# Second attention: the next image's transposes and projections one slot earlier, statistics in slot 10 of the image before

## The reference

```
xn = layer_norm(x) * scale + offset                      # per position, 192 channels
q, k, v = xn @ wq + bq, xn @ wk + bk, xn @ wv + bv       # 12 heads of 48
logits = q @ k.T / sqrt(48) + bias_h(q, rel_pos_0) + bias_w(q, rel_pos_1)
out = softmax(logits) @ v                                # 256 x 256 per head and image
x2 = x + (out @ wo + bo)
```

## Time and profile before

| | us |
|---|---|
| median of three runs (lowest, highest) | 853.67 (852.67, 854.36) |
| the profiled execution, its own time | 853.72 |
| its span, first to last instruction | 851.9 |
| PE busy in the span | 762.1 (89%) |
| DVE busy | 528.4 (62%) |
| ACT busy | 435.5 (51%) |
| POOL busy | 129.8 (15%) |

### The profile page before, as it was taken

How to read it: one execution, slowest core, us unless ns; L and a number is a source line. 1 busy time by engine, 2 the same in 40 slices (tenths; PEclk the granted TensorE clock), 3 DMA queues, 4 the chain that set the end, 5 groups by cost and what they waited for, 6 DMA issues and landing times.

```text
span 851.9 us, 18544 instructions
## 1 busy us (share of the span) xinstructions
PE 762.1 (89%) x6570; PEld 614.5 (72%) x6570; DVE 528.4 (62%) x1592; ACT 435.5 (51%) x1421; POOL 129.8 (15%) x243
## 2 busy tenths in 40 slices
PE   3779889898989887799979999999999999997998
PEld 2557566575756664589967787878787878775998
DVE  6155866767576777567426676766666666675551
ACT  2025655656465564455435555555555555654442
POOL 7200111011010110033330101010101010100221
PEclk9569999999899998799997999999999999999999
DMA  7321621010102100100040404040404040400001
GB/s 142 60 54 31 165 36 21 17 24 14 32 6 37 19 19 1 36 3 1 2 75 1 76 1 75 2 75 1 76 1 76 1 76 1 76 1 1 20 20 38
DMA packets 39147, 30.06 MB, mean 35 GB/s; under 512 B 12662, under 2 KB 37010, under 8 KB 39056
## 3 DMA queue, kind: packets, MB, share of 16 engines
q1 hardware_dynamic: 36030, 26.55, 16.8%
q0 software_dynamic: 2048, 1.89, 1.2%
q10 hardware_dynamic: 978, 0.43, 0.3%
HBM read 8.77 MB, written 1.57 MB: 12 GB/s over the span
## 4 chain that ended last, share of the span: by engine, by line
PE 75%; DVE 12%; issue 4%; ACT 3%; DMA 3%; SPq 1%; ACTq 1%; POOL 1%; DVEq 0%; POOLq 0%
PE bank L1284 10%; PE bank L1370 8%; PE bank L536 7%; PE bank L516 7%; PE bank L1311 5%; PE bank L1159 5%; PE bank L1291 4%; PE bank L966 4%; PE bank L1330 4%; PE bank L990 4%; PE bank L1091 3%; PE bank L1426 3%; DVE Pb L718 3%; DVE nmax L697 2%; PE bank L1017 2%
## 5 line engine op out<-in xcount | busy, mean ns | idle before, releaser
L707 ACT ACTIVATE Pb<-bank,nmax 128x256 f32<-128x256 f32 (+1 forms) x432 | 192.4, 453 | 89.6 <-DVE nmax L697 86.8
L697 DVE TENSOR_REDUCE nmax<-bank 128x2 f32<-128x392 f32 (+2 forms) x240 | 138.7, 579 | 45.2 <-PE bank L1284 33.0
L718 DVE TENSOR_SCALAR Pb<-Pb,rsum 128x196 f32<-128x196 f32 (+2 forms) x432 | 136.8, 354 | 8.5
L737 ACT COPY area<-bank 98x392 f32<-98x392 f32 (+1 forms) x144 | 77.5, 539 | 84.1 <-PE bank L1291 71.9
L1284 PE MATMUL bank<-QK 80*128 80x256 f32 x384 | 107.7, 405 | 9.6 <-DMA QK<-rel_dense 7.4
L1284 PEld LDWEIGHTS bank<-QK 80*128 80x128 f32 x384 | 69.1, 198 | 30.8 <-issue 14.6
L707 ACT ACTIVATION_READ_ACCUMULATOR Pb<-bank,nmax 128x1 f32 x432 | 87.4, 202 | 0.0
L990 PE MATMUL bank<-ident,Pb 128*98 128x128 f32 x384 | 64.2, 292 | 20.7 <-DVE Pb L718 20.7
L525 ACT ACTIVATE area<-bank,fc1b 128x256 f32<-128x256 f32 x96 | 45.2, 476 | 55.7 <-PE bank L516 48.2
L990 PEld LDWEIGHTS bank<-ident,Pb 128*98 128x98 f32 x384 | 41.6, 133 | 35.1 <-DVE Pb L718 29.9
L536 PE MATMUL bank<-fc2w,area 128*128 128x192 f32 x384 | 64.7, 326 | 0.0
(11 more groups left out here) (151 smaller groups left out, 1494.4 us busy)
## 6 DMA issues: line engine op xcount, KB each, us to landing
QK<-dense SPq DMA_DIRECT2D x32, 288.0 KB, 6.2
QK<-dense SPq DMA_DIRECT2D x48, 64.0 KB, 2.4
QK<-dense SPq DMA_DIRECT2D x90, 28.0 KB
QK<-rel_dense SPq DMA_DIRECT2D x32, 48.0 KB, 3.3
QK<-rel_dense POOLq DMA_DIRECT2D x32, 48.0 KB, 3.0
out<-x_all SPq DMA_DIRECT2D x8, 192.0 KB, 2.0
x_all<-in_x SPq DMA_DIRECT2D x1, 1344.0 KB, 17.0
QK<-in_c_hot SPq DMA_DIRECT2D x2, 384.0 KB, 5.0
```

The source lines that it names most:

```text
L697: nc.vector.tensor_reduce(nmax[0:sc.shape[0], u % 3, 0:sc.shape[1]], sc, AX.X, ALU.max, negate=True).then_inc(self.m_rdy, 1)
L707: nc.scalar.activation(Pb[u % 3][0:rows, t, 0:cols], sc[:, t, :], ACT.Exp, bias=nmax[0:rows, u % 3, t:t + 1], accum_out=esum[0:rows, u % 3 ...
L718: nc.vector.tensor_scalar(Pb[u % 3][0:rows, t, 0:keep], Pb[u % 3][0:rows, t, 0:keep], rsum[0:rows, u % 3, t:t + 1], None, ALU.mult).then_i ...
L737: copy(*self.pt_views(u)).then_inc(self.pt[self.pt_engine(u)], 1)
```

## The change

All front work of the second attention from `xhat` on moves one slot forward, in the same lumps: `xhat` into slot 0, the transposes of x and both halves of the normalized x into slot 1, q and k in slots 2, 3 and 4 (the last with the position products), the copies into `rel_dense` in slot 5, v in slots 6 and 7. The statistics move from slot 0 of an image to slot 10 of the image before it, two images ahead of their use; those of image 1 are taken at the start of the stage. POOL makes `rstd` accordingly behind `xbias` of two images before, and no longer ahead of the four DMAs. No instruction is added or taken away. The first attention keeps its order.

```diff
                 slot = {"pe": self.pe_slot, "act": self.act_slot, "dve": self.dve_slot}[which]
+                if which == "dve" and self.STATS_SLOT is not None:
+                    self.dve_stats(eng, Img(0, 1))
                 for k in sorted(fronts):
-                    if started and k <= 2:
+                    if started and k <= self.XT_SLOT:
                         continue
...
-                if u == 2 and ahead(self.NU - 1, 1):
+                if u == self.XT_SLOT and ahead(self.NU - 1, 1):
                     self.pe_transpose_x(eng, n.next())
...
-                if u == 1 and ahead(self.NU - 1, 1):
+                if u == self.XT_SLOT - 1 and ahead(self.NU - 1, 1):
                     self.dve_xhat(eng, n.next())
                 if u == self.VALUES_BEHIND and has_prev:
                     self.dve_back(eng, n.prev())
+                if u == self.STATS_SLOT and 2 * n.pair + n.par + 2 < B:
+                    self.dve_stats(eng, n.next().next())
...
         class Attention1(Attention):
+            XT_SLOT = 1
+            STATS_SLOT = 10
-            V_SLOT = 7
+            V_SLOT = 6
...
-                self.dve_fronts = {0: [self.dve_stats], 1: [self.dve_xhat], 2: [self.dve_xn], 3: each(self.dve_k, (0, 1, 2)),
+                self.dve_fronts = {0: [self.dve_xhat], 1: [self.dve_xn], 2: each(self.dve_k, (0, 1, 2)),
...
+            def run_pool(self, eng, following, after_front):
+                self.norm.pool_rstd(eng, Img(0, 1))
+                self.pool_front(eng, Img(0, 0))
+                after_front(eng)
+
+                def step(n, has_prev, has_next):
+                    if has_next:
+                        self.pool_front(eng, n.next())
+                    else:
+                        following(eng)
+                    self.pool_xbias(eng, n)
+                    if 2 * n.pair + n.par + 2 < B:
+                        self.norm.pool_rstd(eng, n.next().next())
+                image_loop(eng, step)
```

More of the change, by code:

```diff
@@ L924, in build @@
         class Attention0(Attention):
+            XT_SLOT = 2
+            STATS_SLOT = None
             G_USES = (6, 5)
@@ L1518, in setup @@
                 self.xl = sem("a1_xl")
[L1519 to L1524, removed]
@@ L1525, in setup @@
-                self.dve_fronts = {0: [self.dve_stats], 1: [self.dve_xhat], 2: [self.dve_xn], 3: each(self.dve_k, (0, 1, 2)),
-                                   4: each(self.dve_k, (3, 4)), 5: each(self.dve_k, (5,)), 6: [self.dve_rel],
-                                   7: each(self.dve_v, (0,)), 8: each(self.dve_v, (1,))}
+                self.pe_fronts = {1: [self.pe_transpose_x], 2: each(self.pe_qk, (0, 1, 2)), 3: each(self.pe_qk, (3, 4)),
+                                  4: each(self.pe_qk, (5,)) + [self.pe_rel], 6: each(self.pe_v, (0,)),
+                                  7: each(self.pe_v, (1,))}
@@ new lines, in setup @@
+                self.act_fronts = {1: [self.act_xn], 2: each(self.act_q, (0, 1, 2)), 3: each(self.act_q, (3, 4)),
+                                   4: each(self.act_q, (5,)), 5: [self.act_rel], 6: each(self.act_v, (0,)),
+                                   7: each(self.act_v, (1,))}
+                self.dve_fronts = {0: [self.dve_xhat], 1: [self.dve_xn], 2: each(self.dve_k, (0, 1, 2)),
+                                   3: each(self.dve_k, (3, 4)), 4: each(self.dve_k, (5,)), 5: [self.dve_rel],
+                                   6: each(self.dve_v, (0,)), 7: each(self.dve_v, (1,))}
@@ L1695, in _ @@
                 nc.gpsimd.memset(v[:, :, :, D1:64], 0.0).then_inc(prep_pool, 1)
-            a1.run_pool(pool, following=lambda e: m1.norm.pool_rstd(e, Img(0, 0)), started=True,
+            a1.run_pool(pool, following=lambda e: m1.norm.pool_rstd(e, Img(0, 0)),
                         after_front=lambda e: m1.low_weights(e, nc.gpsimd))
```

## The result

The changed kernel took **846.97 us** in the median of 10 runs (845.11 to 851.35), against 854.42 of the kernel before on the same chip in 10 runs (852.67 to 858.14): ratio 0.991, with a 95% interval of 0.989 to 0.9929. Its profiled execution took 846.04 us, with a span of 844.2 (before: 853.72 and 851.9); PE is busy for 756.5 us of it (90%).

The account below looks back on a forecast made before the run. PE's instruction stream plus its waits was taken to bound the second attention. Terms -5.4, -0.7, +1.8 and +0.1 sum to -4.2 on 853.72, giving 849.5 us; range 847.8 to 853.2.

Parts of the forecast that it names:

- signs: Profile after: no slot 9 waits, some 0.3 us at q, 41.5 us between images, DVE's wait about 0.5, clock 1.00.
- Slot 9, -5.4: Slot 9's scores: all seven waits, put down to late scatters out of rel_dense, go, saving 5.4 us.
- 0.3 to 0.9 early: Slot 9: scatters that came 0.44 to 1.03 us late would come 0.3 to 0.9 us early.
- The new wait at q, +1.8: q behind the values: PE waits 0.3 us in each of six images for a 2.7 us chain from residual to q.
- Sequence costs, -0.7: PE's order of scores and products: one costlier case fewer per image, -0.1 us for each of seven images.
- xhat: xhat in slot 0 on DVE, ahead of PE's transposes of x: cost 0, bounds 0 to 0.1 us for seven images.
- statistics: Statistics in slot 10 on DVE: 1.0 us covered by 1.46 us of idle time, cost 0.
- the start: Start of the stage: image 1's statistics ahead of the first copy of k cost +0.1 us, bounds 0 and 0.4.
- POOL against DVE: DVE's norm colliding with POOL's xbias moves a slot forward; 1.1 us remain before the transposes, so cost 0.
- The longer chain: Rival: wait at q of 0.7 to 1.0 us in six images, 851.9 to 853.7 us; chance 14%.
- a kept wait in slot 9: Rival: slot 9's wait stays in part, through exponentials or late landings, 850.5 to 852.5 us; chance 8%.
- The clock: Rival: pauses at q drop PE's granted clock, up to 859.7 us; slower by pause or clock, chance 8%.

Follow-up runs that it names:

- e9: Kernel before, with the q and k transfers issued in two parts, heads 0 to 5 as soon as copied: 845.7 us, ratio 0.9894.
- e2: The changed kernel, unchanged, run again beside the kernel before: 849.12 us, ratio 0.9947.
- e12: The changed kernel with only 48 added transposes of the identity on PE in image 0's wait: 846.59 us, ratio 0.9899.
- e6: The changed kernel with the statistics back in slot 0 ahead of xhat and POOL's order as before: 871.36 us, ratio 1.018.
- e1: The kernel before, unchanged, run again beside itself: 855.9 us, ratio 1.002.
- e5: The kernel before, with ACT copying its half of rel_dense at the end of slot 5, not 6: 854.56 us, ratio 0.9992.
- e8: Changed kernel with DVE's half of normalized x ahead of the previous image's residual, plus 48 identity transposes in image 0's wait: 842.15 us, ratio 0.9845.
- e10: Changed kernel with DVE's half of normalized x ahead of the previous image's residual and q and k transfers in two parts: 840.8 us, ratio 0.9827.
- e11: Changed kernel with DVE's normalized x ahead of the previous residual, q and k transfers in two parts, 32 identity transposes: 841.45 us, ratio 0.9834.

## Why the prediction was right or wrong

**What bounds the kernel.** Right: PE's stream and its waits. A period of after is 41.23 us; of before, less its wait in slot 9, 41.20. Most signs that it named came too: DVE's wait before copying head 11's transposes fell from 1.46 us to 0.62, and the mean from slot 9 to slot 9 is 41.4 us, where 41.5 was forecast. None of them could tell its mechanism from the one below.

**Slot 9, -5.4.** The amount was right (5.46 to 0), and so was counting all seven alike. That the exponentials were not what held the three named images is shown by the landings in the trace of before (0.25 us ahead of the scores in these three as in the others), and by e9, which left the exponentials where they were: of 1.03, 0.96 and 0.44 there, 0.84, 0 and 0 are left, and the profile puts the 0.84 down to the scatters. The **mechanism was wrong**. I read the scatters' issue and landing, and not what else was in the DMA engines. The margin came from q and k being issued farther ahead of slot 9: 13.24 us in after (512.45 to 525.69), where before would have had 12.15 without the wait and the scores can start about 12.9 us behind that issue. "0.3 to 0.9 early" was too much by this count, since the wait removed was itself up to 1.03 and only 1.09 us came in between, not the 1.3 reckoned. What made the right sum come out of the wrong reason is that the change moves q, k and scatters by the same distance.

**The new wait at q, +1.8.** Place, releaser and count were right, and so was the sum of 2.7 us for the chain. It measured 1.2 by the waits and 1.6 from start to start, 0.2 to 0.27 an image against 0.3.

**Sequence costs, -0.7.** This is the term of the sum that was furthest off. Before and after differ by +0.03 in an unwaited period (41.20 and 41.23), and after contains 0.2 to 0.27 at q. So the sequence gave -0.17 to -0.24 in each of six images, -1.0 to -1.4. Why it gave so much wasn't tried.

**xhat, statistics, the start, POOL against DVE.** All at 0 to within 0.1 as far as the profiles show, and the start's +0.1 did not come: from arrival to the first q issue there are 8.39 us in both. For those under way: image 0 takes 73.56 us from arrival instead of 74.29, which is its slot-9 wait and 0.03. A norm that met POOL's `xbias` took 1.23 us in after instead of 1.97, and no wait of PE follows it.

**Sum.** Predicted -4.2, measured in the stage -5.6. Slot 9 gives -5.46. The other edits were to cost +1.2 and cost +0.2, six times 0.03 (image 0's 0.03 goes the other way). The last -0.3 are delays that come once, as the prediction had expected of the image at 661 us: an excess of 0.83 in one period of before, of 0.52 in one of after.

**Why 847.0 fell out of the range.** Two steps failed. The first is the size of two terms, the wait at q and the sequence costs: together they were to cost 1.1 us (+1.8 and -0.7) and cost 0.2 (six times 0.03). With the 0.3 of delays that come once and the start's 0.1 this is the step from -4.2 to -5.6. It alone would give 848.1, still inside. The second is the range itself, "the range 847.8 to 853.2 ... leaves a little room below". It was built from the bounds of the edits and took the median before as fixed: "nothing is to be corrected". But 2.06 us of the two profiles' difference arose ahead of the stage, where the programs do the same and the clock was 0.60 before and 0.84 after (42 to 64 us). The medians of one program also differ between measurements, 846.97 and 849.12 of the changed one, 853.49 to 856.42 of the kernel before. A range of edits from 848 needed about 2 us on each side for that. That the first measurement fell out and the second would have lain inside is chance.

**The rivals.** The longer chain did not come, nor did a kept wait in slot 9. The clock did not fall behind 0.2 us at q. But that the length of the pause decides "between 1.03 us ... and 2.01" was wrong: e2 lost the clock behind 1.02, e12 kept it behind 1.01, and of e6's six pauses of 1.75 it fell behind two. The Trainium skill ("TensorE: Matmul & The Clock Gate", section "A second HAM failure mode: psum-queue depth-cycling") tells of clock swings behind frequent short idles. This trace shows none behind six waits of 0.2 us, at a clock of 1.00; but with one such wait in 41 us they are not frequent, so it hardly tests that.

## What to carry to other kernels

When a wait is put down to a DMA, look at what fills the DMA engines between issue and landing before moving the issue. A constant distance from an earlier, larger transfer points to its volume as the bound, and here issuing the first half of it as soon as it was ready gave as much as the rearranged schedule. When a wait is put down to an engine that was long done, compare the landings of the DMAs with the start of what waited. A move can be worth nothing alone and still be what another move needs, so undo it inside the change as well as trying it by itself. Give a forecast's range the spread of medians of the unchanged program, not only the bounds of the edits.

## What was not expected of the hardware

- The same pause of PE is or isn't followed by half clock: behind 1.01 us in e1, 1.02 in e2 and twice 1.15 in e5 it was, behind 1.01 in e12 and 1.08 and 0.92 in e8 it wasn't, and behind e6's 1.75 it was two times of six.
- All fourteen programs do the same in the first 40 us, yet eight profiles show a mean clock of 0.77 to 0.79 there (before and e1 among them) and six 1.00 (after, e2 and e5 among them). Arrivals at the second attention range from 424.5 to 427.5 us in the six and from 426.2 to 431.4 in the eight, so the clock in the first 40 us is not all of it. What decides it stays open.
- Nine of the fourteen profiles have a pause of 0.3 to 1.2 us inside the position products of the last image with a next one, with no releaser; others have one like it in an earlier image or just behind these products. Its cause wasn't tried.
- The scatters, DMAs of 48 KB, took 2.3 to 2.4 us to land in the medians of the stage in e9, e10 and e11, where half of q and k had gone ahead, 3.1 in before and 3.8 in after, where they were issued nearer behind q and k.
